# Layer 1 of two cross-attention layers: the transposed probabilities move from TensorE to a path over HBM, and the output runs two tiles behind the logits

## The reference

```python
a = _layer_norm(audio_kv, ln_gamma, ln_beta)           # the 64 context tokens of each batch
Q = (hidden_states @ Wq.T)   # 16 heads of 64
K = (a @ Wk.T)
V = (a @ Wv.T)
scores = jnp.einsum('bhtd,bhsd->bhts', Q, K) * scale
scores = jnp.where(mask, scores, -inf)
attn = softmax(scores, axis=-1)
out = einsum('bhts,bhsd->bhtd', attn, V) ; out = out @ Wo.T
return hidden_states + jnp.tanh(gate) * out
```

## Time and profile before

| | us |
|---|---|
| median of 3 runs | 1935.14 (1933.84 to 1935.18) |
| the profiled execution: device time | 1932.28 |
| the same execution: span in the profile | 1930.5 |

### The profile page before, as it was taken

One profiled execution on the slowest core, in us unless ns is written; L12 is line 12 of the kernel. 1 busy time (PEld: TensorE's weight loads), 2 busy tenths in 40 slices (PEclk: granted clock), 3 DMA queues, 4 the chain that ended last, 5 costly groups with the idle time before them and its releaser, 6 DMA issues.

```text
span 1930.5 us, 22356 instructions
## 1 busy us (share of the span) xinstructions
PE 1826.7 (95%) x8640; PEld 1509.4 (78%) x8640; DVE 1082.6 (56%) x1086; ACT 585.9 (30%) x680; POOL 1032.3 (53%) x580
## 2 busy tenths in 40 slices
PE   5999999999988899999999977999999999999998
PEld 5788888888876777888778856887788778877887
DVE  6888888888867444444344456335633563356342
ACT  3444444444434332233332323112211221122111
POOL 2677777777758755465544656225522552255221
PEclk9999999999999999999999989999999999999999
DMA  8423333233163475655756554422342234132110
GB/s 204 108 76 82 83 79 78 74 81 85 45 191 111 131 235 201 198 180 175 242 188 211 189 189 153 152 77 83 136 153 66 100 118 153 66 118 101 66 55 33
DMA packets 249961, 244.43 MB, mean 127 GB/s; under 512 B 61440, under 2 KB 204928, under 8 KB 249856
## 3 DMA queue, kind: packets, MB, share of 16 engines
q1 hardware_dynamic: 248704, 241.97, 39.9%
q10 hardware_dynamic: 1152, 1.05, 0.2%
HBM read 157.99 MB, written 84.93 MB: 126 GB/s over the span
## 4 chain that ended last, share of the span: by engine, by line
PE 56%; DVE 19%; issue 9%; ACT 6%; POOL 4%; DMA 3%; SPq 2%; ACTq 0%; DVEq 0%; POOLq 0%
PE ps L53 18%; PE ps L55 18%; PE ps L54 18%; DVE small L972 4%; DVE pr L995 3%; ACT pr L741 3%; DVE pT1r L1006 2%; DVE pT0r L1006 2%; PE ps L648 2%; ACT ot L735 2%; DVE xT0r L902 1%; DVE xT1r L902 1%; POOL prob L1280 1%; DVE x2r L1075 1%; DMA xb<-in_x_dram 1%
## 5 line engine op out<-in xcount | busy, mean ns | idle before, releaser
L1275 POOL TENSOR_TENSOR prob<-prob,small 128x1024 f32<-128x1024 f32 x32 | 61.0, 1908 | 397.0 <-DVE small L1086 397.0
L1206 POOL TENSOR_TENSOR pr<-pr,small 128x1024 f32<-128x1024 f32 x64 | 122.0, 1906 | 100.0 <-DVE small L1001 100.0
L1082 DVE SCALAR_TENSOR_TENSOR prob<-ps,bias 128x1024 f32<-128x1024 f32 x32 | 39.1, 1222 | 227.6 <-PE ps L55 227.6
L840 ACT CAST x2Th<-x2r 128x1024 fp32r<-128x1024 f32 x32 | 33.6, 1050 | 424.6 <-DVE x2r L1075 424.6
L1227 POOL TENSOR_TENSOR xb<-xb,bo 128x1024 f32<-128x1024 f32 x32 | 79.9, 2497 | 141.0 <-DMA xb<-in_x_dram 141.0
L1201 POOL TENSOR_TENSOR pr<-pr,small 128x1024 f32<-128x1024 f32 x64 | 124.0, 1938 | 34.8 <-DVE small L976 34.6
L1050 DVE TENSOR_TENSOR y<-ps,xb 128x512 f32<-128x512 f32 x64 | 44.0, 687 | 159.3 <-PE ps L55 156.4
L972 DVE TENSOR_REDUCE small<-pr 128x16 f32<-128x1024 f32 x64 | 78.1, 1220 | 91.0 <-ACT pr L741 91.0
L53 PE MATMUL ps<-wo0h,oc0l 128*128 128x512 f32 x256 | 101.6, 397 | 0.0
L53 PE MATMUL ps<-wo0h,oc1l 128*128 128x512 f32 x256 | 101.0, 395 | 0.0
L53 PE MATMUL ps<-xT0h,wq0l 128*128 128x512 f32 x256 | 100.7, 393 | 0.0
(11 more groups left out here) (320 smaller groups left out, 5583.1 us busy)
## 6 DMA issues: line engine op xcount, KB each, us to landing
o_scratch<-ot SPq DMA_DIRECT2D x256, 64.0 KB, 1.8
ocr<-o_scratch SPq DMA_DIRECT2D x16, 1024.0 KB, 6.2
xb<-in_x_dram SPq DMA_DIRECT2D x32, 512.0 KB, 6.0
x_scratch<-y SPq DMA_DIRECT2D x32, 512.0 KB, 3.5
a_scratch<-ost SPq DMA_DIRECT2D x64, 256.0 KB, 3.0
b_scratch<-ost SPq DMA_DIRECT2D x64, 256.0 KB, 2.5
xd<-x_scratch SPq DMA_DIRECT2D x128, 128.0 KB, 2.8
raw<-b_scratch SPq DMA_DIRECT2D x32, 512.0 KB, 8.0
```

The source lines that it names most:

```text
L1206: nc.gpsimd.tensor_tensor(heads(v), heads(v), mx.unsqueeze(2).to_broadcast([P, TPB * GRP, KEYS]), ALU.subtract)\
L1275: nc.gpsimd.tensor_tensor(prob[:], prob[:], mx1.unsqueeze(2).to_broadcast([P, H1, KEYS]), ALU.subtract)\
```

## The change

In layer 1 the probabilities are no longer transposed on TensorE. SyncE stores `prob` to a scratch area in HBM (one DMA of 512 KB), waits until that has landed, and loads it back in the folded form as `pd` (four DMAs of 128 KB). VectorE transposes `pd` in 32x32 blocks into `probr`, ScalarE casts the high part from there, and GpSimd (before: VectorE) makes the low part. `probr` and the transposed parts now exist twice; `PT` is gone, and `xt` has two buffers where it had four. The rows of B are taken in another order to fit the fold (`piece`).

The order of all engines changes with it. TensorE makes the logits of tile u and then the output of tile u-2. The logits of tiles 0 and 1 now stand ahead of the half tiles 62 and 63. On each of VectorE, ScalarE and GpSimd a tile's iteration now begins with the transposed probabilities of the tile before; VectorE turns the next tile's x2 ahead of the softmax, not within it. The new A is still split at m = 7, the new B at m = 1 instead of m = 0, and the raw A is loaded at m = 3. The masks, the gate and the tanh move from the last half tiles to half tile 16.

```diff
@@ sync
+            def turn_prob(u):
+                sp.wait_ge(probs1, u + 1)
+                sp.dma_start(d["p"][u % 2], prob[:].rearrange("p h s -> p (h s)")).then_inc(p1_st, 16)
+
+            def load_pd(u):
+                sp.wait_ge(p1_st, 16 * (u + 1))
+                after(sp, p1_turned, u)
+                for a in range(4):
+                    sp.dma_start(pd[32 * a:32 * (a + 1)], d["p"][u % 2, :, 256 * a:256 * (a + 1)]
+                                 .rearrange("(t j) c -> j t c", t=TPB)).then_inc(pd_ld, 16)
...
                 elif m == 0:
                     for c in range(KT):
                         load_raw(1, b, c)
-                if u + 2 < NTILE:
+                if 1 <= u and u + 2 < NTILE:
                     load_xd(u + 2)
-                if m == 2 and b + 1 < BATCH:
+                if m == 3 and b + 1 < BATCH:
                     for c in range(KT):
                         load_raw(0, b + 1, c)
...
+                if u:
+                    turn_prob(u)
+                    load_pd(u)
+                if u >= 2:
+                    store_out(u - 2)
+                    if u < NTILE:
+                        sp.wait_ge(stored[(u - 2) % 4], 16 * ((u - 2) // 4 + 1))
+                        load_xt(u)
@@ tensor
-                    if u == UNITS + SLOTS - 2:
-                        logits(0)
+                    if u >= UNITS + SLOTS - 2:
+                        logits(u - (UNITS + SLOTS - 2))
                     half_tile(u - UNITS)
...
-            turn_prob(0)
-            for u in range(1, NTILE):
+            for u in range(2, NTILE):
                 logits(u)
-                output(u - 1)
-                turn_prob(u)
+                output(u - 2)
+            output(NTILE - 2)
             output(NTILE - 1)
@@ scalar
             def prob_hi(u):
                 act.wait_ge(p1_turned, u + 1)
...
+                after(act, o1_done, 2 * (u - 1))
+                nc.scalar.copy(probT[u % 2][0][:], probr[u % 2][:]).then_inc(p1_hi, 1)
...
+            for u in range(2, NTILE):
                 b, m = divmod(u, KT)
...
+                prob_hi(u - 1)
+                if m == KT - 1 and b + 1 < BATCH:
+                    for c in range(KT):
+                        split_ab(0, b + 1, c)
+                if u + 1 < NTILE:
+                    split_x2(u + 1)
+                exponential(u)
+                if m == 1:
                     for c in range(KT):
                         split_ab(1, b, c)
+            prob_hi(NTILE - 1)
@@ vector
+            def turn_prob(u):
+                dve.wait_ge(pd_ld, 64 * (u + 1))
+                after(dve, o1_done, 2 * (u - 1))
...
+                nc.vector.transpose(probr[u % 2][:].rearrange("p k (t j) -> p t k j", t=TPB),
+                                    pd[:].rearrange("p t (i k) -> p t k i", k=KT)).then_inc(p1_turned, 1)
@@ gpsimd
+            def prob_lo(u):
+                pool.wait_ge(p1_hi, u + 1)
+                nc.gpsimd.tensor_tensor(probT[u % 2][1][:], probr[u % 2][:], f32(probT[u % 2][0][:]), ALU.subtract).then_inc(p1_lo, 1)
...
+            for u in range(2, NTILE):
                 b, m = divmod(u, KT)
+                prob_lo(u - 1)
                 if m == KT - 1 and b + 1 < BATCH:
                     for c in range(0, KT, 2):
                         low(0, b + 1, c)
-                center(u)
                 if u + 1 < NTILE:
                     split_x2(u + 1)
+                center(u)
                 scale(u)
-                if m == 0:
+                if m == 1:
                     for c in range(0, KT, 2):
                         low(1, b, c)
+            prob_lo(NTILE - 1)
```

More of the change, by code:

```diff
@@ L389, in load_raw @@
                     sp.wait_ge(*lo_done(c, b if which else b - 1, 1 - which))
-                sp.dma_start(raw[c][:], piece(d["b" if which else "a"][b], c)).then_inc(ab_ld[c // 2], 16)
+                sp.dma_start(raw[c][:], piece(which, b, c)).then_inc(ab_ld[c // 2], 16)
             def stored_x2(u):
@@ L403, in load_xt @@
                 stored_x2(u)
-                sp.dma_start(xt[u % 4][:], d["x2"][P * u:P * (u + 1), :]).then_inc(x_ld[u % 4], 16)
+                sp.dma_start(xt[u % 2][:], d["x2"][P * u:P * (u + 1), :]).then_inc(x_ld[u % 4], 16)
             def prepare(h):
+                if h == 8:
+                    for i in range(2):
+                        sp.wait_ge(o_st[i], 64 * UNITS // 2)
+                    sp.dma_start(km[:], d["km"].rearrange("b s -> (b s)").rearrange("(o n) -> o n", o=1)
+                                 .to_broadcast([P, BATCH * KEYS])).then_inc(c1_ld, 16)
+                    sp.dma_start(gate, d["gate"].rearrange("(o n) -> o n", o=1).to_broadcast([P, 1])).then_inc(c1_ld, 16)
                 if h == SLOTS - 8:
@@ L442, in layer1 @@
                         load_raw(1, 0, c)
-                    for v in range(4):
+                    load_pd(0)
+                    for v in range(2):
                         load_xt(v)
@@ L636, in output @@
                     for k in range(2):
-                        last = three(nc, O1[n], [probT[x][:, 2 * q + k] for x in (0, 1)],
+                        last = three(nc, O1[n], [probT[u % 2][x][:, 2 * q + k] for x in (0, 1)],
                                      [B[x][c][:, k] for x in (0, 1)], q == 0 and k == 0, q == 3 and k == 1)
@@ L642, in output @@
                         last.then_inc(b_free, 1)
-            def turn_prob(u):
-                pe.wait_ge(probs1, u + 1)
-                after(pe, p1_lo, u)
-                for k in range(KT):
-                    last = nc.tensor.transpose(PT[:, P * k:P * (k + 1)],
-                                               prob[:, 2 * k:2 * k + 2, :].rearrange("p h s -> p (h s)"), ident[:])
-                last.then_inc(p1_turned, 1)
             for u in range(UNITS + SLOTS):
@@ L1112, in prepare @@
                     turn_x2(0)
-                if h == SLOTS - 3:
-                    low(0, 0, 5)
+                if h == 16:
                     dve.wait_ge(c1_ld, 32)
@@ L1120, in prepare @@
                         nc.vector.copy_predicated(bias[:, b], km[:, b], zero[:]).then_inc(set_, 1)
+                if h == SLOTS - 3:
+                    low(0, 0, 5)
                     dve.wait_ge(set_, 2 + BATCH)
@@ L1300, in gpsimd @@
                     prepare(u - UNITS)
-                if u == UNITS + SLOTS - 2:
-                    scale(0)
+                if v >= 0:
+                    scale(v)
             beta(NTILE - 1)
-            for c in range(0, KT, 2):
+            for c in (0, 2, 4):
                 low(1, 0, c)
-            for u in range(1, NTILE):
+            prob_lo(0)
+            low(1, 0, 6)
+            for u in range(2, NTILE):
                 b, m = divmod(u, KT)
+                prob_lo(u - 1)
                 if m == KT - 1 and b + 1 < BATCH:
```

137 lines of the change are left out of this document (62 added, 75 removed).

## The result

| | before | after |
|---|---|---|
| median | 1935.16 (4 runs, 1933.84 to 1935.49) | 1956.39 (4 runs, 1951.84 to 1958.99) |
| the profiled execution: device time | 1932.28 | 1958.99 |
| the same: span in the profile | 1930.5 | 1957.2 |

The ratio of after to before is 1.0108 (95% interval 1.0088 to 1.0129): the change makes the kernel 21 us slower. The profiled execution of after is the slowest of its four, 2.6 us above the median.

The account below looks back on a forecast made before the run. TensorE bounds the kernel, busy 702.84 of 727 us. Output 0's end 1218 + 60 passes 653.6 + edges 66.4 + end 4.5 = 1942.5 against a span of 1930.5; forecast 1945 us, range 1914 to 1976.

Parts of the forecast that it names:

- m = 7: Batch edge, new A split behind the probabilities: TensorE waits 11.7 us and loses 2.4 at the clock, 14.1, three times.
- m = 1: New B's split delays x2's low part: 1.7 us wait plus 1.9 clock, three times; raw B's store meeting adds 0.4, no stop.
- m = 3: Probabilities' store queued behind the raw A loads: 2.1 us wait plus 1.9 clock in batches 1 and 2, 5.3 in batch 0.
- 61 passes and the tail: From output 0 on: TensorE's passes, each one logits or one output at 10.9 us, and the span's tail; 668.5 us.
- What the change takes away: Layer 1 on TensorE: 27.8 us of transpositions and every wait for `scale` go; with nothing late, 21.8 us per tile.
- The loop: From T, start of turning one x2, through store and load of probabilities to the next T: 21.0 us against TensorE's 21.8.
- the long-loop rival: Store-and-load cycle longer than TensorE's period, deciding from 21.8 us: lateness 5.0 before every edge, 1980 us; chance 0.17.
- The end: Last tile of layer 1: 0.5 us of waiting, for its low part.
- The clock: TensorE's granted clock drops after waits: 1.9 us lost after each short wait, about 2.4 after a long one.
- The start: Passage from layer 0: two waits and a late `pd` replace what early logits gain; output 0 starts 1205.3, ends 1218.
- The cheap edges: Rival: VectorE and GpSimd don't slow each other, edge costs shrink from 66.4 to about 25, 1904 us; chance 0.18 including milder form.
- no late edge: Rival: nothing late at any batch edge, only if A were split ahead of `pd`: 1879 us; chance 0.03.

## Why the prediction was right or wrong

The direction was right and the time lies in the range (1914 to 1976), but the step was half of what it should be: plus 10 forecast, plus 21 measured. The mechanism was the one described; the loop's slack was sized too large, and several smaller terms too small. From output 0 on, by the terms of the sum (the profiled execution, us):

| term | predicted | measured |
|---|---|---|
| output 0 starts | 1205.3 | 1203.98 |
| waits at the three edges | 35.1 | 36.5 |
| waits at m = 1 (with one of 0.3 elsewhere) | 5.1 | 9.4 |
| waits at m = 3 | 7.6 | 10.6 |
| waits at the end | 0.5 | 4.4 |
| clock after waits | 20.4 | 20.1 |
| 61 passes and the tail | 668.5 | 672.3 |
| the span's end | 1942.5 | 1957.2 |

The measured loss at the clock is the sum of (1 - granted clock) times the length, over stretches of 3 us behind each wait; the last row but one is what remains of 1957.2 - 1203.98.

**What the change takes away: right.** The transpositions and every wait for `scale` are gone, and without the trip the kernel takes 1884 us (the sum without lateness said 1879).

**The loop: 21.0 predicted, 21.3 to 21.5 measured, and this is the step that failed.** `prob` is ready at T + 12.5 (12.3 predicted), the store takes 2.60 (2.85), the load 4.2 to 4.4 (3.75), each turning 2.05 (2.15). The load is the one mis-sized part: my bounds were 3.7 and 4.1 and I took the low end, on the argument that the first of four issues would be the slowest; it is over the high end. It is a small error with a long arm. The loop works off 0.3 to 0.5 us of lateness per tile instead of 0.8, so a lateness of one place arrives at the next. At T6, the turning of x2 ahead of tile 7, I had put 1.3 us of it. Measured it was 4.2: tile 6's logits end at 1298.8, and T6 is 1303.06. Tile 7's logits end at 1320.6 (1264.43, five passes and the clock's 1.8), and `pd` is turned at 1322.38, 1.8 us after that end, where I had it 1.7 before. At the other two edges the lateness was 2.0 and 4.0, and `pd` came 1.3 and 3.3 us later than in the sum. That is near the state that I gave the long-loop rival (5.0 before every edge, 1980 us), though the loop is still just below the period. The doubled load shows how near: 4.2 us per tile more cost 4.1. Over the three edges the late `pd` is 8.1 us, the largest error in the sum; it is hardly seen in the table, since another error hid it.

**m = 7: 11.7 and 2.4 predicted, 12.2 and 2.6 measured on the mean, partly by luck.** `pd` came 1.3 to 3.5 us later than in the sum, and the low parts were 1.9 too long in it: I gave four of them 3.34 each, 13.4, and they take 11.5 (1327.54 to 1339.01), since the first starts before GpSimd's and the second is led by the cast. So 8.1 us too little stand against 5.8 too much. The kernels with A first and with all low parts on VectorE confirm the reading: 12.96 fell to 2.89 by the order, to 10.73 by the engine.

**m = 3: 2.1 to 3.4 predicted, 2.9 to 4.5 measured.** The store behind the raw burst did take the place of the slow output store: it landed 16.5 us after the burst's start, predicted 16.8. In batch 0 the tile behind it was slower too, T to T 23.1 with a store of 4.38, which I had not counted; in the other two batches that store took 2.80 and 2.60. The late raw loads took nearly all of these waits away.

**m = 1: 1.7 predicted, 2.7 measured; the step "the raw B also meets a store, but at its very end: 0.4, no stop" was wrong.** The store of the probabilities there takes 5.99 us, 3.4 more than a plain one, and the tile takes 24.8 from T to T. The raw B is followed by `xd`, whose four issues took 3.49 us instead of 1.74, and the store is issued 13.2 us after the burst's start. I had set the end of the burst by the time of landing in a free queue. The low parts in VectorE's list, which the prediction did count, are still the larger share: the tile behind takes 25.6 us from T to T, 4.2 more than a plain one. Three times 0.33 for `B6l` come on top, which I had not put in.

**The end: 0.5 predicted, 4.4 measured.** Two outputs follow each other with no logits between them. The first waits for VectorE to add the output before (`finish` at 1925.84, which stands behind the softmax of tile 31 in its list), the second for the last probabilities, which need the whole trip. I had looked at the second alone, and there at a low part.

**The clock: right in sum, wrong in its parts.** I gave each short wait 1.9. The granted clock of the 6 us behind four waits of the changed kernel:

```profile
1264.00:1270.00 6.00, 5.57 (x17) 4.47 (x18) 2.61 (x4) 1.06 (x1) 3.29 (x3) 0.72 0.00 0
1344.00:1350.00 6.00, 5.41 (x13) 4.26 (x14) 2.45 (x4) 1.06 (x1) 3.29 (x3) 0.50 0.06 16
...
1416.00:1422.00 6.00, 5.67 (x25) 4.71 (x26) 2.69 (x4) 1.06 (x1) 3.29 (x3) 1.00 0.00 0
1464.00:1470.00 6.00, 5.34 (x14) 4.22 (x15) 2.38 (x4) 1.06 (x1) 3.29 (x3) 0.55 0.01 3
```

By the length of the pass behind it, the wait of 2.94 us cost 1.8 us, that of 12.96 cost 2.6, that of 4.51 cost 2.4, and the one of 2.68 at 1416.34 nothing to speak of.

**The start: the time was right, the judgment wrong.** Output 0 began 1.3 us before my 1205.3, and all of that is tile 0's logits, which began 1.4 us earlier in this execution. But "the early logits buy little" left out what they cost: the kernel with one early tile is 9.0 us faster. I had followed the start to output 0 alone and not to the first turning of the steady loop, which is 7 us later for them and from which the lateness is handed on. About half of the gain is such lateness; 2.9 us are the clock at output 0.

**61 passes and the tail: 3.8 us more.** A plain pass takes 10.88 us, not 10.89, which is 0.6 us less in all. But in front of each of the 15 waits behind output 0's start a pass takes 0.16 us more, 2.4 us that the sum did not have, and in the stretch behind each edge, where the new B comes in piece by piece, six passes take 66.0 to 66.3 us after waits and clock instead of 65.4, another 1 to 2 us. The rest, about 1 us at most, I can't place.

**The rivals.** The cheap edges did not happen (12.2 us each): VectorE and GpSimd do slow each other, 3.3 us for a pair. With A split ahead of `pd`, which the prediction named as the condition for no late edge, the edge waits fall to 2.6 to 3.3 us, but the time only to 1929 and not to 1879. The loop did not grow longer than the period, 21.4 against 21.8. The rule of the Trainium skill that speaks for TensorE's transposition ("VectorE: DVE Perf Modes", section "Rules for kernel authors") gives no verdict here: the detour loses as it is built, 1956 against 1935, and with the same DMAs, other lists and the low parts on VectorE the kernel takes 1894.

## What to carry to other kernels

When a step leaves an engine for a longer way round, work out the loop that it closes (from one use of the single buffer to the next) and set it against the bound engine's period: here 21.4 against 21.8, so that the margin, and not the length of the way, decided what every other delay cost. Follow a lateness from the place where it arises to the next place where something is late, with the measured loop and not with the nearest lower bound. And put work that has no deadline (a 4 MB burst, the split of the next batch's operands) behind what the loop waits for in the queue or ahead of what the loop can't deliver yet on an engine: these moves of a few lines, with the low parts on VectorE alone, turned 21 us of loss into 42 us of gain.

## What the runs showed of the hardware

- A store of 512 KB to HBM that takes 2.60 us takes 5.95 to 8.25 us behind eight loads of 512 KB whose issue began 8.6 to 13.2 us before it on the same queue; where the burst is issued late, behind the tile's own store, the next tile's store takes 4.7 to 4.9 us at m = 3 and 4.0 to 4.3 at m = 1.
- VectorE's subtraction of two arrays in SBUF takes 1.21 us alone (one each 1.14) and 3.35 beside GpSimd's; eight of them took 10.5 us on VectorE alone at an edge, and 13.8 on both, from the first start to the last end.
- In the eleven changed kernels' traces no wait of TensorE ahead of a pass, from output 0 on and the last pass aside, costs more than 0.2 us at the clock if it is below 1.87 us, every wait from 2.94 us up costs 1.5 to 3.0 us, and those between do one or the other (the pass behind the wait, less 10.88). Of the three waits of 2.7 us at m = 1, one cost 1.8 us and two nothing in the changed kernel, and the same in the kernel with one early tile; TensorE had run some 70 us without a pause over 0.6 us before each, and I have no rule for it.
